# Attention and gated FFN on one core: conversion and statistics work placed in pieces among the tiles, the row step set apart, two FFN groups' snapshots first

## What is computed

```python
def _L0_attn_ref(x, qkv, o_proj, gamma, beta):          # x is already layer-normed once
    x_norm = (x - mu) / jnp.sqrt(var + EPS) * gamma + beta
    q, k, v = x_norm @ qkv[:, :512], x_norm @ qkv[:, 512:1024], x_norm @ qkv[:, 1024:]
    scores = jnp.einsum('bsk,btk->bst', q, k) / sqrt(512)
    attn = softmax(where(causal, scores, -inf))
    return (attn @ v) @ o_proj + residual

def _L0_ffn_ref(x, w_gate, w_up, w_down):
    h = silu(x @ w_gate) * (x @ w_up)
    h_sparse = _sparsify_2to4(h)      # of each 4 neighbours, the 2 largest in magnitude stay
    return h_sparse @ w_down

xn = _layernorm(x)
x = x + _L0_attn_ref(xn, ...) + _L0_ffn_ref(xn, ...)
```

## Time and profile before

| | |
|---|---|
| runs of the kernel before | 873.73, 876.32, 877.72 us; median 876.32 |
| the profiled execution | 875.79 us, its span 874.0 us |
| PE busy / PE weight loads | 825.3 us (94%) / 672.0 us (77%) |
| DVE / ACT / POOL busy | 578.8 (66%) / 314.1 (36%) / 13.7 us (2%) |
| granted TensorE clock, mean | 0.974 of full speed |
| DMA | 117.03 MB, 134 GB/s on the mean |

### The profile page before, as it was taken

The page is one execution under the profiler, slowest core; times in us unless marked ns, Lnnn a source line. Parts: engine busy times, 40 slices in busy tenths (PEclk is TensorE's granted clock), DMA queues, the critical chain, the costliest instruction groups (busy, mean ns, idle before and its releaser), DMA issues. The chain is left out here.

```text
span 874.0 us, 9524 instructions
## 1 busy us (share of the span) xinstructions
PE 825.3 (94%) x3635; PEld 672.0 (77%) x3635; DVE 578.8 (66%) x985; ACT 314.1 (36%) x514; POOL 13.7 (2%) x33
## 2 busy tenths in 40 slices
PE   5897998999799989799999999999999999999997
PEld 4775886888588878687877887887888888888875
DVE  6657376435533335576879979879676668558796
ACT  5414224111311221456443553445334325234431
POOL 2010110000000000000000000000000000000000
PEclk9898999999899999999999999999999999999998
DMA  9331153110100204446445237564527442351002
GB/s 325 132 125 68 61 165 113 73 37 25 61 12 25 73 13 143 206 169 266 194 179 215 97 169 262 210 266 178 206 85 277 178 169 63 154 212 53 1 0 97
DMA packets 30012, 117.03 MB, mean 134 GB/s; under 512 B 2912, under 2 KB 2960, under 8 KB 27536
## 3 DMA queue, kind: packets, MB, share of 16 engines
q1 hardware_dynamic: 25792, 108.83, 33.4%
q10 hardware_dynamic: 4176, 7.60, 2.5%
HBM read 74.45 MB, written 41.97 MB: 133 GB/s over the span
## 5 line engine op out<-in xcount | busy, mean ns | idle before, releaser
L597 PE MATMUL bank<-X_hi,wset 128*128 128x512 f32 x448 | 178.5, 398 | 8.7 <-DVE X_lo L919 4.4
L599 PE MATMUL bank<-X_hi,wset 128*128 128x512 f32 x448 | 176.6, 394 | 0.0
L598 PE MATMUL bank<-X_lo,wset 128*128 128x512 f32 x448 | 176.6, 394 | 0.0
L597 PEld LDWEIGHTS bank<-X_hi,wset 128*128 128x128 f32 x448 | 85.5, 191 | 32.8 <-ACT bank L794 7.9
L599 PEld LDWEIGHTS bank<-X_hi,wset 128*128 128x128 f32 x448 | 85.4, 191 | 18.2
L598 PEld LDWEIGHTS bank<-X_lo,wset 128*128 128x128 f32 x448 | 85.6, 191 | 17.4
L679 PE MATMUL bank<-dw,hs_hi 128*128 128x512 f32 x224 | 87.7, 392 | 0.8 <-DVE acc L1097 0.3
L680 PE MATMUL bank<-dw,hs_hi 128*128 128x512 f32 x224 | 87.2, 389 | 0.0
L681 PE MATMUL bank<-dw,hs_lo 128*128 128x512 f32 x224 | 87.1, 389 | 0.0
L1097 DVE TENSOR_TENSOR acc<-bank,acc 128x512 f32<-128x512 f32 x64 | 43.4, 687 | 51.6 <-PE bank L681 51.6
L473 PE MATMUL bank<-v_hi,pT_hi 128*128 128x512 f32 x136 | 56.6, 416 | 12.8 <-DVE pT_lo L887 12.6
(11 more groups left out here) (165 smaller groups left out, 1410.3 us busy)
## 6 DMA issues: line engine op xcount, KB each, us to landing
w_operands<-wset SPq DMA_DIRECT2D x8, 3584.0 KB, 12.0
wset<-w_operands SPq DMA_DIRECT2D x8, 3584.0 KB, 11.6
wsum<-w_units SPq DMA_DIRECT2D x28, 256.0 KB, 3.3
dw_raw<-L_ffn_w_down SPq DMA_DIRECT2D x14, 512.0 KB, 4.8
xw<-L_attn_x SPq DMA_DIRECT2D x4, 1024.0 KB, 9.8
xt_raw<-x_t SPq DMA_DIRECT2D x8, 512.0 KB, 6.8
xn_t<-xt_raw SPq DMA_DIRECT2D x8, 512.0 KB, 2.8
X_raw<-xn_t SPq DMA_DIRECT2D x8, 512.0 KB, 4.8
```

The costliest lines, as they stand in the source:

```text
L597: pe.matmul(dst[:], u[:, 0, :], x_hi, start=(first and kt == 0), stop=False, skip_group_check=True)
L598: pe.matmul(dst[:], u[:, 0, :], x_lo, start=False, stop=False, skip_group_check=True)
L599: last = pe.matmul(dst[:], u[:, 1, :], x_hi, start=False, stop=(kt == 1), skip_group_check=True)
```

## The change

No operation is added or taken out but for semaphores and waits. The list of steps and a few functions are put in another order:

- **Start.** Chunk 0's factors (`x_scale`, `x_rows`) come after the last weight splits, `vo_weight` 0 and 1 ahead of `x_turn`, and `x_turn` is done in two halves, the second behind `vo_weight` 2. `v[0][0]` goes ahead of `scores` 0.
- **Chunk work.** `xn` of chunk 0 moves from tile 0 to tile 4; both `xh_pre` of chunk 1 go to tile 0 and its four `xh` to tile 1; `v[1][0]` to tile 2; statistics of chunk 2 and 3 go among the `z` products; chunk 2's and 3's `xh` and `xn` are taken apart. A new table `behind` hangs work after `attend`.
- **Row step.** The two operations on `rows` become a step of their own, `rows`, behind `attend` and `behind`.
- **Last tile.** `X_first` and `X_second` go ahead of the pT_lo of the third key group, `X_third` and `X_fourth` right behind it.
- **W operands.** Two of the four hi halves of the first weight set go behind tile 13's `attend`, the other two, with two lo halves, behind tile 14's.
- **FFN.** For n = 2 and n = 8 the first two snapshots (`seeds`) come ahead of the four magnitudes on ACT; `down_hi(0)` goes from the end of group 1 to its middle.
- Waits and one buffer (`xt_raw` of chunk 2) follow these moves.

```diff
     steps += [*stat[0], x_stats[0], x_rstd[0], qk[0], qk[1], split[2][0], split[3][0], qk[2], split[2][1], split[3][1], qk[3],
-              xw_load[2], xt_load[1], split[2][2], split[3][2], x_scale[0], ("x_rows", 0, 0), split[2][3], split[3][3],
-              ("x_turn", 0, 0), vo[0], vo[1], *xh_pre[0], vo[2], xh[0][0], stat[1][0], xh[0][1], stat[1][1], vo[3], xh[0][2], stat[1][2],
+              xw_load[2], xt_load[1], split[2][2], split[3][2], split[2][3], split[3][3], x_scale[0], ("x_rows", 0, 0), vo[0], vo[1],
+              ("x_turn", 0, 0), *xh_pre[0], vo[2], ("x_turn", 0, 1), xh[0][0], stat[1][0], xh[0][1], stat[1][1], vo[3], xh[0][2], stat[1][2],
...
-              z[0][3], row_spread[1], ("scores", 0, 0), exp[0], v[0][0], xn[0][0], v[0][1], xn[0][1], xn_store[0]]
+              z[0][3], row_spread[1], v[0][0], ("scores", 0, 0), exp[0], v[0][1]]
...
-    beside = {0: [v[0][2], xh_pre[1][0]],
-              1: [xh_pre[1][1], v[0][3], *xh[1][0:2]],
...
+    beside = {0: [v[0][2], *xh_pre[1]],
+              1: [*xh[1], v[0][3]],
+              2: [v[1][0]],
...
-        steps += [*beside.get(i, []), ("attend", i, 0)]
+        steps += [*beside.get(i, []), ("attend", i, 0), *behind.get(i, []), ("rows", i, 0)]
...
-                        act.wait_ge(xn_ready[1], 2)
+                        act.wait_ge(xn_stored[2], 32)
...
+                if n in (2, NQ):
+                    seeds(n)
+                    magnitudes(i)
+                else:
+                    if i >= 0:
+                        magnitudes(i)
+                    seeds(n)
...
+                if n == 1:
+                    down_hi(0)
                 if i >= 0:
                     kept_hi(i)
...
                 elif kind == "attend":
-                    slot = n % 2
-                    for g in groups_of(kind, n):
-                        probs_lo(n, g)
-                    ...
                     if n == NT - 1:
                         X_first(0)
                         X_second(0)
-                        X_third(0)
-                        X_fourth(0)
+                    for g in groups_of(kind, n):
+                        probs_lo(n, g)
+                        if n == NT - 1 and g == HEAD:
+                            X_third(0)
+                            X_fourth(0)
...
+                elif kind == "rows":
```

More of the change, by code:

```diff
@@ L77, in attention_ffn @@
[L77 to L86 removed]
+    between = {3: [*xn[1], xn_store[1], xt_load[2], z[1][1], *stat[2], x_stats[2], x_rstd[2], z[1][2], z[1][3], v[1][1]],
+               7: [z[2][0], *stat[3], x_stats[3], x_rstd[3], xt_load[3], *z[2][1:4], v[2][0]],
+               11: [z[3][0], xn[3][0], z[3][1], xn[3][1], xn_store[3], *z[3][2:4], v[3][0]]}
@@ L87, in attention_ffn @@
+    beside = {0: [v[0][2], *xh_pre[1]],
+              1: [*xh[1], v[0][3]],
+              2: [v[1][0]],
+              3: [x_scale[2]],
+              4: [v[1][2], row_turn[2], row_store[2], *xn[0], row_spread[2], xn_store[0]],
+              5: [v[1][3], *xh_pre[2], xh[2][0]],
+              6: xh[2][1:4],
+              7: [x_scale[3], xn[2][0]],
+              8: [v[2][1], row_turn[3], row_store[3], row_spread[3]],
+              9: [v[2][2]],
+              10: [v[2][3], *xh[3][0:2]],
               11: [v[3][1]],
@@ L88, in attention_ffn @@
               12: [*v[3][2:4], ("w_load", 0, 0)],
-              13: [("w_sum", 0, 0), *fills("w_hi", 0)],
-              14: fills("w_lo", 0)}
+              13: [("w_sum", 0, 0)],
+              14: fills("w_lo", 0)[0:2]}
+    behind = {8: [xn[2][1], xn_store[2]],
+              9: xh_pre[3],
+              10: xh[3][2:4],
+              13: fills("w_hi", 0)[0:2],
+              14: [*fills("w_hi", 0)[2:4], *fills("w_lo", 0)[2:4]]}
     for i in range(NT):
@@ L544, in _ @@
                 elif kind == "x_turn":
-                    for i, row in enumerate((2, 3, 0, 1)):
+                    for i, row in ((0, 2), (1, 3)) if k == 0 else ((2, 0), (3, 1)):
                         pe.wait_ge(rows_wide_ready, i + 1)
@@ L746, in _ @@
                     if n == 3 and k == 0:
-                        act.wait_ge(xn_ready[1], 2)
+                        act.wait_ge(xn_stored[2], 32)
                     nc.scalar.copy(xT_hi[n][:, k, :], h).then_inc(xh_hi_ready, 1)
-                elif kind == "x_turn":
+                elif kind == "x_turn" and k == 1:
                     act.wait_ge(rows_turned, 4)
@@ L807, in last_silu, with seeds, magnitudes @@
                 nc.scalar.activation(g_sum[1][:], g_sum[1][:], ACT.Silu).then_inc(silu_ready, 1)
+            def seeds(n):
+                snapshot(0, n, F_P1, bank[0], bank[2], 4 * (n - 1) + 1 if n else 0, 0)
+                snapshot(1, n, F_P1, bank[1], bank[3], 0, 0)
+            def magnitudes(i):
+                act.wait_ge(down_full, TC * i)
+                for r in range(G):
+                    if r % 2 == 0:
+                        act.wait_ge(hid_ready, 4 * (2 * (i // 2) + r // 2 + 1))
+                    magnitude(i, r)
             for n in range(N_Q):
                 i = n - 2
-                if i >= 0:
-                    act.wait_ge(down_full, TC * i)
-                    for r in range(G):
-                        if r % 2 == 0:
-                            act.wait_ge(hid_ready, 4 * (2 * (i // 2) + r // 2 + 1))
-                        magnitude(i, r)
-                snapshot(0, n, F_P1, bank[0], bank[2], 4 * (n - 1) + 1 if n else 0, 0)
-                snapshot(1, n, F_P1, bank[1], bank[3], 0, 0)
+                if n in (2, NQ):
[5 more added lines that the diff above has]
+                    seeds(n)
                 act.wait_ge(full[0], FILLS * n + F_P2)
@@ L1046, in _ @@
                 elif kind == "attend":
-                    slot = n % 2
-                    for g in groups_of(kind, n):
-                        probs_lo(n, g)
-                    dve.wait_ge(rows_loaded[slot], 16 * (n // 2 + 1))
-                    rows_scaled = step(nc.vector.tensor_scalar(rows[:, slot, :], rows[:, slot, :], one_rstd[:, n:n + 1],
-                                                               neg_mean_rstd[:, n:n + 1], ALU.mult, ALU.add))
                     if n == NT - 1:
@@ L1063, in _ @@
                             X_lo_half(0, i)
+                elif kind == "rows":
+                    slot = n % 2
+                    dve.wait_ge(rows_loaded[slot], 16 * (n // 2 + 1))
+                    rows_scaled = step(nc.vector.tensor_scalar(rows[:, slot, :], rows[:, slot, :], one_rstd[:, n:n + 1],
+                                                               neg_mean_rstd[:, n:n + 1], ALU.mult, ALU.add))
                     dve.wait_ge(vec_step, inverse_made)
```

24 lines of the change are left out of this document (7 added, 17 removed).

## The result

| | before | changed |
|---|---|---|
| runs (us) | 873.73 to 877.72, median 875.03 (4) | 838.86 to 840.95, median 839.71 (4) |
| ratio to before | | 0.959, 95% interval 0.956 to 0.962 |
| profiled execution (span) | 875.8 (874.0) | 840.95 (839.2) |
| busy share PE, DVE, ACT | 94%, 66%, 36% | 97%, 69%, 37% |

A forecast was written before the change was run, and what follows sets the result against it. PE was taken to set the end, its waits (34.7 us) and lower clock (16.5) limiting any gain to 51 us. Terms A to I summed to 33.2 us, 875.8 to 842.6; the median 0.5 above gave 843.0 us (832 to 856).

The forecast's parts named there:

- A: Start to v[0][1]: PE's waits and lost clock of 10.6 us go, 2.6 us of new waits come; gain 8.0 us.
- B: Tiles 0 to 3: 10.0 us go, 5.3 of waits and 2.0 of clock come; gain 2.7 us (-1 to +6).
- C: z of chunk 2: one strip goes to tile 5, 1.9 us of wait stay; gain 1.4 us (0 to 3.3).
- D: Tile 9: PE's wait goes, since xh_pre[3] stands behind the pT_lo that PE waits for; gain 0.8 us.
- E: Tile 10: two strips and all of xn[3] leave the place ahead of the third group's pT; gain 8.6 us.
- F: Tile 13: ACT's four copies of W go behind pT_hi, removing a wait and its clock; gain 4.3 us.
- G: Start of the FFN: DVE's sums of X end before the pT_lo is wanted; wait and clock go; gain 6.9 us.
- H: FFN, n = 2: snapshots precede magnitudes, but the wait moves to DVE's chain; gain 0 us (-1 to +3.3).
- I: FFN, n = 8: ACT's wait goes, DVE's sum decides, the clock may take some; gain 0.5 us (-0.5 to +3.2).
- R1: FFN waits at n = 2 and 8 paid back in full: 6.1 us more than the sum, 837 us; chance 0.15.
- R2: Tiles 0 to 3 give nothing, the clock stays low and chunk 1's strips come later: 849 us; chance 0.16.
- R4: FFN: DVE's lag from the moved seeds is handed on through 13 groups, 45.5 us, 888 us; chance 0.01 with anything else slower.

## Why the prediction was right, and where it was not

- *What bounds the kernel.* Right. Every gain and every loss in these kernels is a wait of PE, the clock behind one, or a start that comes late. The reading that 0.231 us is PE's pace was slightly off: starts stand 0.227 us apart, and a group of 132 matmuls takes 29.92 us without a wait (group 2 of the kernel with DVE's sums first), 30.67 in groups 3 to 6 and 30.26 from group 9 on, where the timeline shows no idle time. The 0.3 to 0.8 us in each group are starts that come late without an idle time being shown: in group 4 of the changed kernel one matmul starts 0.44 us and one 0.50 us behind the one before. By the prediction's own last sentence another pace is a sign of being wrong; over the 60 matmuls of its longest use here it comes to 0.2 us. PE's starts also show that each wait costs 0.27 us more than its idle time (last section), so the 51 us said to be the most that could be gained were too few, by an estimated 3.5 us (13 waits of 0.27).
- *A.* 8.03 us for 8.0. The size was right, the account of it in part. The waits that came are 0.61 us at z[0] (0.7 said) and 0.64 at row_turn (0.9 said); the parts that the prediction names make 2.2 us and not its 2.6. And with the rest as changed, 7.5 us hang on the place of the transposes, z[0]'s wait among them, because a DVE queue behind the split of vo_weight 1 held xh_pre[0]; the prediction doesn't name that queue.
- *B.* 4.7 us for 2.7, inside its range; the step that was off is the clock. The wait at attend 1 was 2.15 us for 1.6, outside the 1 to 2 said, and that at v[1][0] 1.64, outside the 2 to 4. From attend 1 to v[1][0] ACT's chain took 8.2 us for the 8.5 worked out, but PE's own work in it took 6.4 us in place of 4.9, since the clock fell between them. So the slower matmuls filled a wait that was there anyway: 1.64 us were left of 3.6. The prediction counted the wait in full and the clock's 2.0 us on top of it. The kernel with the row's half first shows the other case: there the clock fell behind v[1][0]'s wait and not ahead of it, the wait was 2.94 us, and attend 3 came 1.6 us later than in the changed kernel, though the code there is the same. Stretches of PE in that kernel:

```profile
66.00:70.00 4.00, 3.45 (x16) 1.00 0.00 0
74.00:78.00 4.00, 4.00 (x12) 0.57 0.17 66
```

- *C.* -0.3 us for 1.4, outside its range of 0 to 3.3. The mechanism was right (z[2] 1.33 us earlier, 2.07 us of wait left for 1.9), but the clock fell behind this wait of 2.07 us, where it had not fallen behind the old one of 3.29. Term C had no clock in it, because the kernel before showed none there:

```profile
150.00:158.00 8.00, 7.37 (x32) 1.00 0.50 185
```

That was one execution, taken for a rule: of the eleven kernels here with this wait (2.06 or 2.07 us), the clock fell in ten.
- *D, E, F, G.* 1.1, 8.3, 4.6 and 7.15 us for 0.8, 8.6, 4.3 and 6.9. Right in size; both parts of E, and F, were undone and cost what they should. D was not undone by itself. G was right as a sum of other parts than named.
- *H, I.* +1.06 and -0.3 us for 0 and 0.5, inside their ranges, and for the reason given: the wait moved to DVE's chain. The size of H was short by the clock, which did not fall. Which way the clock would go there was luck: it fell in group 8. Over all terms the misses of B and H (+3.1) and of C and I (-2.5) nearly cancel, and how close the profiled 840.95 us came to the sum's 842.6 owes something to that.
- *The rivals.* R1 wanted the waits of the FFN to vanish; 0.81 + 1.63 + 2.11 us of them stand in the rows above. R2's late chunk 1 and R3's late loads did not come. R4's lag was not handed on: groups 3 to 6 take 30.7 us each and group 7 30.3, in both kernels. So a group isn't the 23 us that R4 was worked out with, and DVE's free time in one is 4.8 us (15.6% of 30.7) and not 3.6, which makes the case against R4 stronger.

## What to carry to other kernels

Undoing one part at a time shows whether an engine waits for a place in a queue or for an amount of work. In this kernel it was mostly the place: two edits of DVE's and ACT's order, which move no instruction to another engine, were worth 4.95 and 3.28 us. In group 8 it was the amount, and the new order gave nothing. Ask of each moved step not only what it displaces on its own engine, but which instruction ahead of it in that queue waits for someone else (here a store, a split, a row load). Count the clock only where PE's next point isn't set by another engine, and count it as a chance, not as what one profile happened to show: here for waits of 1.8 us and up.
